# Gated cross-attention and FFN on one core: an own order of units for each engine, work moved off VectorE, and two batches' ctx turned in 32x32 blocks

## Chip, cores, metric

One core of one Trainium2 chip. The metric is device time in microseconds for one launch, the median of three runs. Engines: PE is TensorE (PEld its weight loads), DVE is VectorE, ACT ScalarE, POOL GpSimd, SP SyncE, which here only issues DMAs.

## What is computed

`x` has 4 batches of 256 tokens with 256 features, `ctx` 4 batches of 1601 rows of 256. Cut to what matters:

```python
h = layernorm(x)                                   # no scale or shift, eps 1e-5
scores = einsum('bsd,bmd->bsm', h, ctx) / sqrt(256)
scores = where(mask, scores, -1e30)
x = x + tanh(g_xattn) * (softmax(scores) @ ctx)    # zero where a batch has no valid row
a = e4m3(layernorm(x))
f = gelu(a @ e4m3(w_gating[0])) * (a @ e4m3(w_gating[1]))     # 256 -> 1024, bf16
x = x + tanh(g_ffn) * (e4m3(f) @ e4m3(w_linear))   # 1024 -> 256
```

## The kernel before

The 1024 tokens are 8 tiles j of 128, two per batch b. The ctx rows of a batch are 12 tiles of 128 and a tail of 65 rows; groups g = 0, 1, 2 hold four tiles each, g = 3 the tail. Both attention products are exact enough only if float32 values are split: `hi` is the value rounded to fp32r (a copy on ACT), `lo` the rest (value minus hi). Each product is then three: hi x hi, hi x lo, lo x hi.

All work is cut into units named by a letter and indices, in one written list (START, MIDDLE once per middle batch, END). Every engine walks this same list and does its own part of each unit, waiting on semaphores for the others:

- G, F, K: layernorm statistics of a batch (DVE), the power -0.5 (POOL, line 320), the normed `xn` (DVE, line 428, two per batch).
- R, Z: ctx group rounded by ACT (line 376, `chl` first half); its rest by POOL (line 334, second half, 1024 columns in one instruction).
- X, C, T: fills of a ring of three PSUM banks. PE transposes 128x128 pieces of `xn`, ctx or the probabilities through the identity (line 580); ACT evicts the bank rounded (line 369), DVE evicts the rest (line 436). C b:0 to b:5 are the six 512-column pieces of a batch (group times 2 + half of the features), C b:6 the tail.
- S j:c: score chunk c of tile j on PE (lines 595, 600, 601), six matmuls of 512 columns for c = 0, 1 and of 290 or 288 for c = 2, 3. M j:h: DVE adds the mask bias and takes the maximum of a half row (line 446, 1024 or 577 columns).
- E j:h: exponential on ACT (line 382). V j:g: probabilities times ctx on PE into bank `pv`: per ctx tile one matmul of 512 columns, hi against [hi | lo] (line 615), and one of 256, lo against hi (line 619).
- A: DVE adds the halves of the row sum (`rt`, line 463), inverts it, forms the factor `fo` (line 465) and adds both halves of `pv` to x (lines 467, 469).
- U, Q, L, N: second layernorm of a tile: statistics on DVE, power on POOL (line 326), the normed e4m3 values on DVE (line 479), N transposes (line 578) and DVE eviction (line 486).
- B: the mask turned to a bias on POOL (lines 311, 314), in an order that follows the ctx rows (row p x 12 + t sits on partition p of tile t).
- W, I: a 1024-column weight chunk rounded to the e4m3 grid: DVE makes the grid step (lines 496, 497), POOL adds and subtracts it (lines 342, 343). Six chunks: 0 to 3 gating, 4 and 5 linear.
- H 0 to 15: FFN hidden units (PE line 654, gelu on ACT line 394, product on DVE line 503); Y 0 to 7: projection (line 668) and final sum (DVE line 508).

`cn` (ctx as loaded) and `chl` exist twice, the turned ctx once. SP issues its DMAs in one fixed order; the loads of batch 2 wait for `c_lo` of batch 0.

Of the kernel before, what the change touches and what calls it, by code (L numbers as in the profile page):

```python
# [5 lines left out]
def gated_cross_attention_ffn(  # L6
# [55 lines left out]
    START = """
        G0 F0 B0 K0 R0:0 C0:0 C0:1 C0:2 X0 C0:3 C0:4 G1 S0:0 C0:5 C0:6 S0:1 F1 Z0:0 S0:2 S0:3 B1 M0:0 K1
        M0:1 G2 R0:1 Z0:1 E0:0 S1:0 G3 C1:0 S1:1 E0:1 T0:0 M1:0 S1:2 X1 R0:2 Z0:2 S1:3 T0:1 M1:1 T0:2
        V0:0 C1:1 R0:3 Z0:3 W0 E1:0 T0:3 V0:1 C1:2 C1:3 V0:2 R1:0 I0 Z1:0 F2 A0 C1:4 C1:5 R1:1 Z1:1 V0:3  # L80
        R1:2 Z1:2 C1:6 W1 E1:1 R1:3 Z1:3 I1 F3 B2 U0"""
# [9 lines left out]
    two_a_batch = "SMETVAUWI"

    def steps(text, batches=0):

        items = [(w[0], *(int(v) for v in w[1:].split(":"))) for w in text.split()]
        items = [(s[0], s[1] + batches * (QT if s[0] in two_a_batch else 1)) + s[2:] for s in items]
        return [s for s in items if s[0] != "B" or s[1] < B]
# [615 lines left out]
```

## Time and profile before

| | us |
|---|---|
| Median of three runs (lowest, highest) | 151.02 (150.79, 151.37) |
| Span of the profiled execution | 149.9 |
| PE busy | 130.0 |
| DVE busy | 126.9 |
| POOL busy | 74.8 |
| ACT busy | 71.2 |

The time beside the profiled execution's span is taken as the median, which lies 1.1 us above it. Busy time is the sum of an engine's instructions in the span; a DVE or POOL instruction that has started and then stands still counts as busy. In the rows, "x" is a count, the first pair after "|" is busy us in all and mean ns of one, then comes the idle time before the group and what ended it. Chain rows read: start, duration in us, what.

### The profile page before, as it was taken

The numbers are of one execution on the slowest core, as the hardware profiler recorded it, in microseconds if no ns is written. First come the engines' busy times: TensorE is split into PE (matmuls) and PEld (weight loads), VectorE is DVE, ScalarE is ACT, GpSimd is POOL, SyncE is SP. The second block draws the span as 40 slices with busy tenths as digits, with TensorE's granted clock in tenths as the row PEclk, the third lists the DMA queues.
The fourth block names the chain that finished last, engine by engine and source line by source line (L and its number), as shares of the span: only waits on it lengthen the run. The fifth ranks groups of instructions, "written<-read, shape, count | busy, mean of one in ns | idle before, by whom it ended". The sixth has DMA issues, their size and how long they took to land.

```text
span 149.9 us, 2277 instructions
## 1 busy us (share of the span) xinstructions
PE 130.0 (87%) x786; PEld 106.3 (71%) x786; DVE 126.9 (85%) x255; ACT 71.2 (47%) x131; POOL 74.8 (50%) x52
## 2 busy tenths in 40 slices
...
PEclk9978999999999999999699999995999999999999
...
GB/s 41 219 376 385 377 145 4 0 165 350 124 0 0 179 413 42 4 0 17 123 0 7 133 0 4 2 0 0 0 4 0 2 0 0 0 4 0 35 115 130
DMA packets 6754, 12.75 MB, mean 85 GB/s; under 512 B 852, under 2 KB 4696, under 8 KB 6744
## 3 DMA queue, kind: packets, MB, share of 16 engines
...
q10 hardware_dynamic: 288, 0.00, 0.1%
q14 instruction: 4, 0.03, 0.1%
...
## 4 chain that ended last, share of the span: by engine, by line
PE 50%; DVE 36%; DMA 5%; issue 4%; ACT 2%; SPq 1%; DVEq 0%
PE ring L580 12%; PE pv L615 11%; PE scores L654 7%; DVE act L428 6%; PE pv L619 6%; DVE wc L497 5%; DMA cn<-in_ctx_dram 5%; DVE wc L496 5%; DVE pT_lo L436 4%; PE ring L668 4%; DVE sp L446 3%; PE scores L600 3%; PE scores L601 3%; PE scores L595 3%; DVE cT_lo L436 2%
## 5 line engine op out<-in xcount | busy, mean ns | idle before, releaser
L334 POOL TENSOR_TENSOR chl<-cn,chl 128x1024 fp32r<-128x1024 f32 (+1 forms) x16 | 31.9, 2006 | 4.0 <-ACT chl L376 3.8
L369 ACT ACTIVATE pT_hi<-ring 128x512 fp32r<-128x512 f32 (+1 forms) x32 | 15.7, 514 | 36.3 <-PE ring L580 36.3
L615 PE MATMUL pv<-chl,pT_hi 128*128 128x512 f32 (+1 forms) x104 | 32.5, 427 | 0.0
L600 PE MATMUL scores<-cT_lo,xT_hi 128*128 128x512 f32 (+2 forms) x64 | 21.9, 350 | 6.6 <-DVE cT_lo L436 6.6
L601 PE MATMUL scores<-cT_hi,xT_lo 128*128 128x512 f32 (+2 forms) x64 | 21.7, 346 | 0.0
L436 DVE TENSOR_TENSOR pT_lo<-ring,pT_hi 128x512 fp32r<-128x512 f32 (+1 forms) x32 | 18.1, 582 | 3.7 <-ACT pT_hi L369 3.7
L619 PEld LDWEIGHTS pv<-chl,pT_lo 128*128 128x128 f32 (+1 forms) x104 | 16.9, 200 | 5.8 <-issue 1.9
L615 PEld LDWEIGHTS pv<-chl,pT_hi 128*128 128x128 f32 (+1 forms) x104 | 19.0, 199 | 2.7
L619 PE MATMUL pv<-chl,pT_lo 128*128 128x256 f32 (+1 forms) x104 | 18.3, 296 | 2.7 <-DVE pT_lo L436 2.7
L382 ACT ACTIVATE sp<-sp,nb 128x1024 f32<-128x1024 f32 (+1 forms) x16 | 15.4, 962 | 9.7 <-DVE nb L452 9.7
L580 PE MATMUL ring<-ident,sp 128*128 128x128 f32 (+1 forms) x104 | 16.5, 285 | 2.8 <-ACT sp L382 2.8
L595 PE MATMUL scores<-cT_hi,xT_hi 128*128 128x512 f32 (+2 forms) x64 | 18.7, 373 | 0.0
L342 POOL TENSOR_TENSOR ws<-ws,wc 128x1024 f32<-128x1024 f32 x6 | 13.0, 2160 | 11.4 <-DVE wc L497 11.4
L436 DVE TENSOR_TENSOR cT_lo<-ring,cT_hi 128x512 fp32r<-128x512 f32 (+1 forms) x28 | 16.7, 626 | 2.3 <-ACT cT_hi L369 2.0
L600 PEld LDWEIGHTS scores<-cT_lo,xT_hi 128*128 128x128 f32 x64 | 12.0, 188 | 8.6 <-DVE cT_lo L436 7.2
L580 PE MATMUL ring<-ident,cn 128*128 128x128 f32 (+1 forms) x104 | 15.4, 285 | 3.0 <-DMA cn<-in_ctx_dram 2.9
L369 ACT ACTIVATE cT_hi<-ring 128x512 fp32r<-128x512 f32 (+1 forms) x28 | 14.5, 550 | 6.4 <-PE ring L580 6.2
L580 PEld LDWEIGHTS ring<-ident,cn 128*128 128x128 f32 (+1 forms) x104 | 13.0, 151 | 4.2 <-issue 3.3
L580 PEld LDWEIGHTS ring<-ident,sp 128*128 128x128 f32 (+1 forms) x104 | 13.1, 147 | 4.0 <-issue 3.3
L326 POOL TENSOR_TENSOR rstd<-ve,half_pow 128x2 f32<-128x2 f32 x4 | 2.8, 698 | 26.1 <-DVE ve L425 26.1
L446 DVE CUSTOM_DVE_ANT_0 sp<-scores,bias 128x1024 f32<-128x1024 f32 (+1 forms) x16 | 15.7, 981 | 0.1
L376 ACT ACTIVATE chl<-cn 128x1024 fp32r<-128x1024 f32 (+1 forms) x16 | 14.3, 899 | 1.2 <-DMA cn<-in_ctx_dram 1.2
...
## 6 DMA issues: line engine op xcount, KB each, us to landing
...
```

Source lines behind the costliest of these rows:

```text
L334: nc.gpsimd.tensor_tensor(chl[b % 2][0:parts, t0:t1, D:2 * D], cn[b % 2][0:parts, t0:t1, :], chl[b % 2][0:parts, t0:t1, 0:D].bitcast(f32), ...
L369: nc.scalar.activation(dst, bank_view(f, size), ACT.Copy).then_inc(hi_ready, 1)
L376: nc.scalar.activation(chl[b % 2][0:parts, t0:t1, 0:D], cn[b % 2][0:parts, t0:t1, :], ACT.Copy).then_inc(c_hi, 1)
L382: nc.scalar.activation(sp[:, j % 2, cols], sp[:, j % 2, cols], ACT.Exp, bias=nb[:, j:j + 1], scale=SCALE, accum_out=rs[:, j, h:h + 1]).the ...
L436: nc.vector.tensor_tensor(dst, bank_view(f, size), hi.bitcast(f32), ALU.subtract).then_inc(freed, 1)
L446: nc.vector.tensor_tensor_reduce(out=sp[:, j % 2, cols], in0=banks[:, at_col:at_col + cols.stop - cols.start], in1=bias[:, b % 2, cols], s ...
L580: last = nc.tensor.transpose(dst, src, ident[0:parts, 0:parts])
L595: nc.tensor.matmul(dst, xT_hi[:, j, k, :], cT_hi[:, k, cols], start=(k == 0), stop=False)
L600: nc.tensor.matmul(dst, xT_hi[:, j, k, :], cT_lo[:, k, cols], start=False, stop=False)
L601: last = nc.tensor.matmul(dst, xT_lo[:, j, k, :], cT_hi[:, k, cols], start=False, stop=(k == KD - 1))
L615: return nc.tensor.matmul(pv[:, :], pT_hi[0:parts, t, :], chl[b % 2][0:parts, t, :], start=(t == 0), stop=(t == NT - 1))
L619: nc.tensor.matmul(pv[:, 0:D], pT_lo[0:parts, t, :], chl[b % 2][0:parts, t, 0:D], start=False, stop=False)
```

## The change

- Each engine gets its own written order of units. SP's order interleaves the loads by ctx group (lower-case letters: x, c, m, w loads, b blocks, o stores).
- DVE to ACT: the first layernorm is now `x` centred only (mean minus x, on ACT), and the factor is applied as scale of the exponential; the second layernorm's values, the N eviction, and the absolute value of a weight chunk times 2^20 (`w_abs`, 1024 columns) go to ACT. The two exponentials of a tile become one of 1601 columns, so `rt` goes.
- DVE to POOL: F is now four small operations, Q three per tile instead of one per batch, and v, the validity factor, one per tile.
- POOL's `chl` rest and weight rounding are issued in 256-column pieces: 4 for a group, 8 for a weight chunk.
- The grid step on DVE is one maximum over 1024 float32 columns instead of two passes over bf16.
- `pv` sums everything in 256 columns: hi x hi and hi x lo are two matmuls of 256 columns; DVE adds `pv` once.
- Batches 2 and 3, groups 0 to 2: instead of six C fills (24 transposes) a second load of ctx, `load_blocks`, puts 32x32 blocks so that one DVE transpose of 32x32 blocks per group (D, 1024 columns) gives the turned ctx; ACT rounds it (1024 columns), POOL forms the rest in four pieces. Their row order changes too, so the bias of these batches is one plain instruction.
- `cn` exists once; group 2 and the tail of `chl` and of the turned ctx exist once, groups 0 and 1 twice. 22 warm-up matmuls instead of 18.

```diff
+    BLOCKED = (2, 3)
...
+    SP_ORDER = steps("""
+        x0 c0:1 c0:0 m0 c0:2 c0:3 x1 c1:1 w0 m1 m2 w1 c1:3 x2 c1:0 c1:2 b2 c2:1 c2:0 w2 m3 w3 b3 c2:3 w4 c2:2
+        c3:0 c3:3 c3:1 w5 c3:2 o3 o0 o1 o2 o4 o5 o6 o7""")
+    ACT_ORDER = steps("""
+        R0:1 C0:3 K0 C0:2 X0 C0:0 C0:1 R0:0 R0:3 C0:5 C0:6 C0:4 J R0:2 K1 W0 C1:2 X1 E0 C1:3 T0:0 T0:1 R1:1 T0:2
+        R1:0 K2 C1:6 T0:3 C1:0 C1:1 W1 C1:5 C1:4 E1 T1:0 T1:2 T1:1 D2:0 X2 E2 W2 D2:1 T1:3 L0 R2:1 T2:1 R1:2
+        T2:0 R1:3 D2:2 T2:3 T2:2 E3 T3:0 R2:0 T3:1 T3:2 K3 C2:6 W3 X3 T3:3 D3:0 E4 D3:1 R2:2 T4:0 R2:3 D3:2 T4:1
+        T4:3 T4:2 L1 R3:0 E5 C3:6 T5:2 T5:1 R3:1 T5:0 T5:3 L2 N0 E6 W4 L3 R3:3 T6:2 T6:0 R3:2 T6:1 E7 T6:3 L4 N1
+        T7:0 H0 T7:1 L5 T7:3 H1 T7:2 W5 L6 H2 N2 H3 L7 H4 H5 N3 H6 H7 H8 H9 H10 H11 H12 H13 H14 H15""")
+    DVE_ORDER = steps("""
+        G0 C0:3 C0:2 X0 C0:0 C0:1 G1 C0:5 C0:4 C0:6 M0:0 M0:1 C1:2 W0 X1 C1:3 G2 T0:0 T0:1 M1:0 T0:2 O0 C1:6
+        M1:1 T0:3 C1:0 C1:1 C1:5 C1:4 A0 W1 M2:0 T1:0 D2:0 D2:1 M2:1 T1:2 U0 T1:1 D2:2 M3:0 O2 X2 T1:3 W2 O1 A1
+        T2:1 T2:0 M3:1 M4:0 T2:3 U1 T2:2 G3 T3:0 A2 D3:0 T3:1 O3 C2:6 T3:2 M4:1 X3 D3:1 M5:0 W3 T3:3 D3:2 T4:0
+        U2 A3 M5:1 T4:3 T4:1 T4:2 M6:0 T5:2 C3:6 T5:1 U3 T5:3 O4 A4 O5 T5:0 M6:1 U4 M7:0 A5 U5 T6:0 M7:1 T6:1
+        T6:2 O6 W4 T6:3 T7:0 A6 H0 O7 T7:1 U6 T7:2 H1 W5 T7:3 A7 U7 H2 H3 H4 H5 H6 H7 H8 H9 H10 H11 H12 Y0 H13
+        H14 Y1 H15 Y2 Y3 Y4 Y5 Y6 Y7""")
+    POOL_ORDER = steps("""
+        Z0:1 B0 F0 Z0:3 Z0:0 Z0:2 B1 F1 F2 v0 I0 Z1:1 Z1:0 v1 I1 D2:0 v2 Q0 B2 D2:1 Z1:2 Z1:3 v3 D2:2 I2 Z2:1
+        Z2:0 Q1 F3 D3:0 D3:1 v4 B3 Z2:3 Z2:2 Q2 v5 D3:2 I3 Q3 Z3:1 Z3:0 Q4 Q5 v6 Z3:2 v7 Z3:3 I4 Q6 Q7 I5""")
+    PE_ORDER = steps("""
+        C0:3 C0:2 X0 C0:0 C0:1 S0:1 C0:5 C0:6 C0:4 S0:0 C1:2 S0:2 S0:3 X1 S1:0 C1:3 S1:1 T0:0 T0:1 S1:3 S1:2
+        T0:2 C1:6 V0:0 V0:1 T0:3 C1:0 C1:1 S2:1 C1:5 C1:4 V0:2 V0:3 S2:0 T1:0 T1:2 T1:1 S2:3 S3:1 S2:2 X2 S3:0
+        V1:0 S3:2 T1:3 T2:1 V1:1 V1:2 V1:3 S3:3 T2:0 S4:1 T2:3 T2:2 S4:0 V2:0 V2:1 V2:2 T3:0 V2:3 T3:1 T3:2 S5:0
+        C2:6 S4:2 V3:0 X3 S4:3 T3:3 V3:1 S5:1 V3:2 S5:3 T4:0 V3:3 T4:1 S5:2 S6:0 T4:2 T4:3 S6:1 V4:0 V4:1 V4:2
+        C3:6 T5:2 T5:1 V4:3 S7:0 T5:0 S6:2 T5:3 S6:3 S7:1 N0 V5:0 V5:1 V5:2 T6:0 V5:3 T6:2 S7:2 S7:3 T6:1 V6:0
+        N1 V6:1 T6:3 V6:2 T7:0 T7:1 H0 V6:3 H1 T7:3 T7:2 V7:0 V7:1 V7:2 V7:3 N2 H2 H3 H4 H5 N3 H6 H7 H8 H9 H10
+        Y0 H11 H12 H13 H14 H15 Y1 Y2 Y3 Y4 Y5 Y6 Y7""")
...
+            def load_ctx(b, g):
+                if b >= 1:
+                    sp_eng.wait_ge(c_lo, pool_z[("Z", b - 1, g)])
+                    if g == NG - 1:
+                        sp_eng.wait_ge(filled, pe_fill[("C", b - 1, KD * g)])
...
+                t0, t1, _ = group(g)
+                rows = ctx_2048[b, 0:NF * P, :].rearrange("(t p) d -> p t d" if b in BLOCKED else "(p t) d -> p t d", t=NF)
+                sp_eng.dma_start(cn[:, t0:t1, :], rows[:, t0:t1, :]).then_inc(c_in[g], 16)
+
+            def load_blocks(b):
+                earlier = [dve_d[s] for s in turns if s[1] < b]
+                if earlier:
+                    sp_eng.wait_ge(turned, max(earlier))
+                src = ctx_2048[b, 0:NF * P, :].rearrange("(m q) (k i d) -> k i q m d", q=Q, k=KD, d=Q)
+                for k in range(KD):
+                    for i in range(P // Q):
+                        sp_eng.dma_start(cb[Q * i:Q * (i + 1), k, :, :], src[k, i]).then_inc(b_in, 16)
...
+                for t in range(t1 - t0):
+                    ins = nc.gpsimd.tensor_tensor(chl(b, g)[0:parts, t, D:2 * D], cn[0:parts, t0 + t, :],
+                                                  chl(b, g)[0:parts, t, 0:D].bitcast(f32), ALU.subtract)
+                ins.then_inc(c_lo, 1)
...
+            def turned_rest(b, g):
+                pool.wait_ge(d_hi, act_d[("D", b, g)])
+                slot = turns.index(("D", b, g)) % 2
+                for k in range(KD):
+                    for a in range(0, BANK, D):
+                        ins = nc.gpsimd.tensor_tensor(cT(b, g, False)[:, k, a:a + D], cr[:, slot, k, a:a + D],
+                                                      cT(b, g, True)[:, k, a:a + D].bitcast(f32), ALU.subtract)
+                ins.then_inc(d_lo, 1)
...
+                pool.wait_ge(wg_ready, dve_w[("W", i)])
+                for a in range(0, HID, D):
+                    ins = nc.gpsimd.tensor_tensor(ws[:, i % 2, a:a + D], ws[:, i % 2, a:a + D], wg[:, a:a + D], ALU.add)
+                link(ins)
+                for a in range(0, HID, D):
+                    ins = nc.gpsimd.tensor_tensor(wq[:, i, a:a + D], ws[:, i % 2, a:a + D], wg[:, a:a + D], ALU.subtract)
+                ins.then_inc(w_ready, 1)
...
+                    ins = nc.scalar.activation(xc[:, j, :], xs[:, j, :], ACT.Identity, bias=mv[:, j, 0:1], scale=-1.0)
...
+            def turned_hi(b, g):
+                wait_ctx_read(actor, b, g)
+                actor.wait_ge(turned, dve_d[("D", b, g)])
+                nc.scalar.activation(cT(b, g, True), cr[:, turns.index(("D", b, g)) % 2, :, :], ACT.Copy).then_inc(d_hi, 1)
...
+            def turn(b, g):
+                n = turns.index(("D", b, g))
+                if g == 0 or turns[n - 1][1] != b:
+                    dve.wait_ge(b_in, 16 * KD * (P // Q) * (sorted(BLOCKED).index(b) + 1))
+                if n >= 2:
+                    dve.wait_ge(d_lo, pool_d[turns[n - 2]])
+                nc.vector.transpose(cr[:, n % 2, :, :],
+                                    cb[:, :, GT * GT * g:GT * GT * (g + 1), :].rearrange("p k m d -> p k (m d)")).then_inc(turned, 1)
...
+            def factor(j):
+                dve.wait_ge(exp_ready, act_e[("E", j)])
+                link(nc.vector.reciprocal(ri[:, j:j + 1], rs[:, j:j + 1]))
+                dve.wait_ge(vt_ready, pool_v[("v", j)])
+                nc.vector.tensor_scalar(fo[:, j:j + 1], ri[:, j:j + 1], vt[:, j:j + 1], None, ALU.mult).then_inc(fo_ready, 1)
+
             def add_attention(j):
-                if j == 0:
-                    dve.wait_ge(tg_ready, 1)
-
-                dve.wait_ge(nb_ready, j + 1)
-                nc.vector.tensor_scalar(vt[:, j:j + 1], nb[:, j:j + 1], 0.5 * NEG * SCALE, tg[:, 0:1],
-                                        ALU.is_lt, ALU.mult)
-                dve.wait_ge(exp_ready, 2 * (j + 1))
-                link(nc.vector.tensor_tensor(rt[:, j:j + 1], rs[:, j, 0:1], rs[:, j, 1:2], ALU.add))
-                link(nc.vector.reciprocal(ri[:, j:j + 1], rt[:, j:j + 1]))
-                link(nc.vector.tensor_tensor(fo[:, j:j + 1], ri[:, j:j + 1], vt[:, j:j + 1], ALU.mult))
-                dve.wait_ge(pv_done, j + 1)
-                link(nc.vector.scalar_tensor_tensor(out=xs[:, j, :], in0=pv[:, D:2 * D], scalar=fo[:, j:j + 1],
-                                                    in1=xs[:, j, :], op0=ALU.mult, op1=ALU.add))
+                dve.wait_ge(fo_ready, dve_o[("O", j)])
+                dve.wait_ge(weighed, pe_weigh[("V", j, NG - 1)])
...
+                nc.vector.tensor_scalar(wg[:, :], wg[:, :], GRID_MIN * 2.0 ** 20, None, ALU.max).then_inc(wg_ready, 1)
...
+                for t in range(t0, t1):
+                    for part in range(2):
+                        nc.tensor.matmul(pv[:, 0:D], pT_hi[0:parts, t, :], ctx[0:parts, t - t0, D * part:D * (part + 1)],
+                                         start=(t == 0 and part == 0), stop=False)
+                pe.wait_ge(freed, dve_lo[("T", j, g)])
+                for t in range(t0, t1):
+                    last = nc.tensor.matmul(pv[:, 0:D], pT_lo[0:parts, t, :], ctx[0:parts, t - t0, 0:D],
+                                            start=False, stop=(t == NT - 1))
+                last.then_inc(weighed, 1)
```

## Rows read from the trace of the kernel before

**Rows 1.** The page: busy us (share of the span); PE's clock in 40 slices.

```profile
PE 130.0 (87%) x786; PEld 106.3 (71%) x786; DVE 126.9 (85%) x255; ACT 71.2 (47%) x131; POOL 74.8 (50%) x52
...
PEclk9978999999999999999699999995999999999999
```

**Rows 2.** The page: chain that ended last, by engine.

```profile
PE 50%; DVE 36%; DMA 5%; issue 4%; ACT 2%; SPq 1%; DVEq 0%
```

**Rows 3.** Groups by line and form, DVE.

```profile
L436 DVE TENSOR_TENSOR cT_lo<-ring,cT_hi 128x512 fp32r<-128x512 f32 x24 | 15.7, 684 | 2.3 <-ACT cT_hi L369 2.0
...
L428 DVE TENSOR_SCALAR act<-xs,mv,rstd 128x256 f32<-128x256 f32 x8 | 10.5, 1353 | 0.8 <-POOL rstd L320 0.8
...
L446 DVE CUSTOM_DVE_ANT_0 sp<-scores,bias 128x1024 f32<-128x1024 f32 x8 | 9.7, 1215 | 0.1
...
L497 DVE TENSOR_SCALAR wc<-wc 128x1024 bf16<-128x1024 bf16 x6 | 8.3, 1379 | 0.2
...
L496 DVE TENSOR_SCALAR wc<-ws 128x1024 uint16<-128x1024 uint16 x6 | 7.3, 1216 | 0.0
...
L463 DVE TENSOR_TENSOR rt<-rs 128x1 f32<-128x1 f32 x8 | 5.6, 698 | 0.0
```

**Rows 4.** Timeline of DVE, 30 to 75 us: start us, us, what.

```profile
34.01 2.00 DVE L465 TENSOR_TENSOR fo<-ri,vt 128x1 f32<-128x1 f32 x1
...
46.13 3.20 DVE L428 TENSOR_SCALAR act<-xs,mv,rstd 128x256 f32<-128x256 f32 x2
```

**Rows 5.** Timeline of POOL, same columns.

```profile
33.84 2.15 POOL L343 TENSOR_TENSOR wq<-ws,wc 128x1024 bf16<-128x1024 f32 x1
...
47.03 2.15 POOL L343 TENSOR_TENSOR wq<-ws,wc 128x1024 bf16<-128x1024 f32 x1
```

**Rows 6.** Chain that ended last, in order of time: start us, us, what.

```profile
51.57 0.47 PE scores L595 x2
...
53.85 0.27 PE scores L595 x2
...
57.85 1.31 PE ring L580 x12
...
59.16 0.93 PE pv L615 x4
...
60.09 0.48 PE pv L619 x4
...
120.04 0.22 PE ring L578 x4
...
127.12 1.74 PE scores L654 x8
```

**Rows 7.** ACT: its timeline to 45 us; then a group by form.

```profile
7.81 1.06 ACT L376 ACTIVATE chl<-cn 128x1024 fp32r<-128x1024 f32 x1 [1.21 <-DMA cn<-in_ctx_dram]
...
L376 ACT ACTIVATE chl<-cn 65x256 fp32r<-65x256 f32 x4 | 1.6, 410 | 0.0
```

**Rows 8.** Groups by line and form, POOL.

```profile
L334 POOL TENSOR_TENSOR chl<-cn,chl 128x1024 fp32r<-128x1024 f32 x12 | 28.9, 2428 | 3.3 <-ACT chl L376 3.3
...
L343 POOL TENSOR_TENSOR wq<-ws,wc 128x1024 bf16<-128x1024 f32 x6 | 13.5, 2249 | 0.5
...
L311 POOL TENSOR_SCALAR bias<-mrow 128x1536 bf16<-128x1536 uint8 x4 | 9.2, 2299 | 6.3 <-DMA mrow<-in_mask_BxS_bk_dram 4.5 <-DVE mx L446 1.6
...
L334 POOL TENSOR_TENSOR chl<-cn,chl 65x256 fp32r<-65x256 f32 x4 | 3.0, 739 | 0.6 <-ACT chl L376 0.5
...
L326 POOL TENSOR_TENSOR rstd<-ve,half_pow 128x2 f32<-128x2 f32 x4 | 2.8, 698 | 26.1 <-DVE ve L425 26.1
```

**Rows 9.** Timeline of SP's queue.

```profile
49.64 1.33 SPq L254 DMA_DIRECT2D cn<-in_ctx_dram  x3
```

**Rows 10.** DMA queues, 0 to 20 us, then 68 to 84 us: packets, MB, share of 16 engines.

```profile
q10 hardware_dynamic: 288, 0.00, 0.7%
...
q1 hardware_dynamic: 1000, 1.01, 22.8%
```

More of the change, by code:

```diff
@@ L91, in gated_cross_attention_ffn @@
[L91 to L97, printed above, removed]
-    order = steps(START) + [s for b in range(B - 2) for s in steps(MIDDLE, b)] + steps(END)
-    fills = [s for s in order if s[0] in "XCTN"]
-    at = {f: i for i, f in enumerate(fills)}
```

569 lines of the change are left out of this document (315 added, 254 removed).

## The prediction

> **What bounds the kernel now.** I read the page first: PE is busy for 130.0 us of the span and DVE for 126.9, so two engines are near full, while ACT (71.2) and POOL (74.8) have room [rows 1]. The chain that ended last agrees: PE half, DVE 36% [rows 2]. A busy DVE is not a working DVE here, though. The `xn` operation of line 428 takes 1353 ns on average for 256 columns, and line 463, one element per partition, 698 ns [rows 3]. The two timelines side by side say why. The one-element `fo` starts at 34.01 and lasts 2.00 us [rows 4]; POOL's 1024-column operation starts at 33.84 and lasts 2.15, so both end at 36.0 [rows 5]. The `xn` pair at 46.13 ends at 49.3, with POOL's operation of 47.03 [rows 4, 5]. DVE stands still until POOL has finished, up to a whole 2.2 us operation.
>
> The Trainium skill ("SBUF — State Buffer", SBUF: two separate sides) calls this an exclusive lock on a port pair, held for a whole instruction and taken by GpSimd and by DVE operations with two SBUF inputs or in a two-port mode. The two pairs of ends agree with it.
>
> PE's own work, at the pace it has when nothing holds it: a transpose 0.109 us (1.31/12), a 512-column score matmul 0.235, a 289-column one 0.135 (0.27/2), a 512-column `pv` matmul 0.233 (0.93/4), a 256-column one 0.12 (0.48/4), an FFN unit 0.87 (1.74/2) [rows 6]. Up to the end of the last attention tile (127.1, where the FFN runs on alone [rows 6]) that is 224 transposes (4 x 26 of ctx, 8 x 13 of probabilities, 16 of `xn`) 24.4, scores 8 x (12 x 0.235 + 12 x 0.135) = 35.3, `pv` 8 x 13 x 0.353 = 36.7, and 2.4 for H0, H1 and three N fills (0.22 each [rows 6]): 98.8 us. The first ctx group is there at 7.8 [rows 7], so in 119.3 us PE lacked 20.5. From 127.1 to the end are 22.8 us, which PE's own 14 FFN units and 64 projection matmuls fill.
>
> **The change part by part.** The sum is against the profiled execution's span of 149.9; the median of the runs, 151.02, is 1.1 above it, and I add that 1.1.
>
> *PE.* 48 transposes (24 each in batches 2 and 3) go: -5.2, leaving 93.6. Splitting the 512-column `pv` matmul into two of 256 costs 2 x 0.12 against 0.233: nothing. Its extra weight loads I cost at nothing too, since the `pT_lo` matmuls load weights before each 256 columns and still run at 0.12 [rows 6]; were it not so, 104 loads would each show. Four more warm-up matmuls lie before the first data.
>
> *DVE.* Gone: 8 `xn` (10.5), 6 mask operations of line 496 (7.3), 8 `rt` (5.6), 12 `cT_lo` evictions (12 x 0.684 = 8.2) [rows 3]; 31.6 in all, and some 36 short ones besides. Added: 6 turns of 1024 columns. No row has a 32x32 turn. Bounds: 0.68, what an eviction of half the columns takes, and 2.4, twice the 1.215 of the 1024-column mask pass; I take 1.2, the same columns [rows 3]: +7.2. The grid operation stays one pass of 1024 (1.38 today [rows 3]), now waiting for at most a 256-column piece. DVE falls to about 100 or less: no longer a bound.
>
> *ACT.* It takes on 16 passes of 256 columns (0.41), 4 of 512 and 6 of 1024 (1.06 each at most) [rows 7]: +6.6 +4.2 +6.4; the 6 turned evictions of 1024 replace 12 of 512. About 88 of 140 us: cover enough.
>
> *POOL.* Here the price is paid. A 1024-column subtraction takes 2.43 us; a 256-column one (on 65 partitions) 0.74 [rows 8]. Four pieces cost between 2.43, if their start-up hides in one another, and 2.96; I take 2.7. Likewise a weight chunk (two passes of 2.2 [rows 8]): 4.3 to 5.4, I take 4.9. Line 320's successor has four small operations, line 326's three per tile; the power takes 0.70 [rows 8] and I give the sets 1.35 and 1.2. In POOL's order, up to the unit Z3:2 that V6:2 waits for: 12 Z x 2.7 = 32.4; three tails 2.2; 6 D x 2.7 = 16.2; 4 masks x 2.5 (2.30 and its tail [rows 8]) = 10.0; 4 F 5.4; four weight chunks 19.6; 6 Q 7.2; 7 v 1.4. Sum 94.4, within about 108 in all against 74.8 now. POOL can start when ScalarE has rounded the first group: 7.8 + 1.06 = 8.9 [rows 7]. I allow 3 us of waiting early (mask, first maxima), so Z3:2 is done at 106.3.
>
> *The sum.* PE has 84.1 us of work ahead of V6:2 by the same prices, so it can be there by 7.8 + 84.1 + 14 of idling, just about in time. From V6:2 it has 9.5 left (V6:2 1.4, T7 1.4, H0 and H1 1.7, the rest of V 5.0), then the 22.8 of the end, which the change leaves as it is: 106.3 + 9.5 + 22.8 = 138.6, and with 1.1 **139.7 us**.
>
> *DMA of the blocks.* Each batch's 1536 rows come again in 128-byte runs, 12288 of them, through 8 DMAs that SP issues at 0.44 each (1.33/3 [rows 9]). Price of a run: a packet of 4 bytes shows as 0.7% of 16 engines in 20 us over 288, 7.8 ns; one of 1010 bytes as 22.8% in 16 us over 1000, 58 ns [rows 10]. Bounds 6.0 us (7.8) and 44.6 us (58) per batch; on the line between, 128 bytes is 14 ns, 10.8 us, which I take, as 128 lies near the small end. Block load 2 is queued behind c1:2, which waits for Z0:2: POOL's sum there gives 21.6. With 3 us of ctx ahead of it and 2 us to land it is there by 37. POOL reaches D2:0 at 42.4 plus 2 of waiting; with turn and eviction ahead, the blocks are wanted at 42. Slack 5 us, or a price of 20.6 ns. Block load 3 waits for D2:2 (about 48, past w3, which waits for I1) and is wanted at 71: slack 10, or 27 ns. At my price both hide. If not, DVE stands at D2:0 with T1:1, U0, M3:0 and all behind it, and ACT and POOL stand behind the same unit.
>
> **The rivals.**
> *A, the pieces are cheap* (2.43 per four, 4.3 per chunk, small operations overlapping): POOL's sum is 9 us less and PE with some 10 us of idling, half of today's, sets the end: 7.8 + 93.6 + 10 + 22.8 + 1.1 = 135. For it: nothing excludes that the start of one piece hides in the piece before; against it: the 65-partition row, far above a quarter of 2.43.
> *B, the waits between engines stay.* PE idles its 20.5 for other reasons than DVE's load (a unit goes PE, ACT, DVE, PE): 7.8 + 93.6 + 20.5 + 22.8 + 1.1 = 145.8. Pieces at 2.96 and 5.4 give nearly the same, 146.4. For it: many hand-offs remain, and in three stretches PE's granted clock falls below its 2.4 GHz (slices at 7, 6 and 5 tenths [rows 1]); against it: DVE had no slack at all to hide a hand-off.
> *C, slower: the blocks come late.* The price of a 128-byte run decides. Total delay is (0.768 p - 15.8) + (0.768 p - 20.8) us, each not below zero, p in ns. It eats the gain of 11.3 at p = 31. At the upper bound, 58 ns, the kernel takes 192. At 33 ns, a run priced as one four times as long on the same line, it takes 139.7 + 9.5 + 4.5 = 154. For it: no row shows a short run from HBM; the 4-byte packets repeat one address. Against it: the price must be more than twice the one read off the line.
> The Trainium skill ("DMA: Bandwidth & Descriptors", Specifications) puts 512 bytes as the least transfer at full rate, since below it the engine reads, modifies and writes. By that rule a 128-byte run costs like a 512-byte one, which is this rival; the trace has no such run to show it.
>
> The skill ("GPSIMD Engine Reference", Engine selection) also advises against two-input elementwise work on GpSimd, as about twice as slow as DVE. The rows bear it out (2428 ns for 1024 columns against 684 for 512 [rows 3, 8], 1.8 times). The change adds 6 units of it, which is why I let POOL set the sum.
>
> **How the numbers follow.** A run-to-run difference below about 0.5% can't be told from none. Chances: the forecast (136 to 143) 0.42; A (131 to 136) 0.18; below 131 0.03; B (143 to 150.2) 0.20; no difference 0.03; C 0.14. Faster 0.83, same 0.03, slower 0.14. The range 131 to 150 leaves out C, no difference and the tail below: 0.20.
>
> **What would show it.** Right: POOL busy over 100 us with hardly a gap between 20 and 105; DVE near 85 to 100 us, no one-element operation above 0.7 us; PE about 5 us less dense work, and waiting for POOL's `chl` or `cT_lo` late in attention; block loads landing within 15 us of issue and DVE's turns near 1.2 us. Wrong: DVE idle ahead of the first turn for a DMA (C); POOL with gaps while PE waits on ACT or DVE (B); a 256-column piece near 0.6 us start to start and PE hardly waiting (A).

## The result, and the profile after

| | time, us (lowest to highest) | ratio to before |
|---|---|---|
| before | 151.19 (150.79 to 152.72) | |
| changed | 146.37 (144.94 to 147.56) | 0.971 [0.964, 0.978] |
| forecast | 139.7 (131 to 150) | |

Faster, as forecast, but by 4.8 us where 11.3 had been forecast. A second measurement gave 147.04 us. The profiled execution is the slowest of its four, 147.56 us with a span of 145.7, and so is that of the second measurement (147.73, span 145.9), both at a mean granted clock of 0.94 where the other six had 0.95 to 0.99 and spans of 143.1 to 145.2, so what is read from these two traces stands for them alone. The time lies 1.8 to 1.9 us above the span in every run here, not 1.1.

The page of the changed kernel: busy time by engine, PE's clock, and the chain that ended last by engine and by line.

```profile
PE 126.3 (87%) x846; PEld 108.0 (74%) x846; DVE 85.0 (58%) x186; ACT 84.6 (58%) x135; POOL 114.4 (79%) x186
...
PEclk9955999999758999999999999999999599999999
...
POOL 67%; PE 21%; DMA 4%; issue 3%; ACT 1%; DVE 0%; SPq 0%; POOLq 0%
POOL chl_a L433 16%; POOL chl_b L433 10%; POOL wq L455 8%; POOL ws L452 8%; POOL cTl_a L444 8%; PE scores L777 7%; PE ring L793 5%; DMA cn<-in_ctx_dram 4%; POOL cTl_b L444 4%; POOL bias L406 3%; PE pv L753 3%; POOL rstd L422 3%; POOL bias L403 2%; POOL sc L394 2%; POOL vt L416 2%
```

DVE went from 126.9 to 85.0 us and left the chain, where it had 36% [rows 1, 2]; POOL went from 74.8 to 114.4 and holds 67% of it (54% in the second profile, with 3% for DVE). PE's busy time fell by 3.7 only, and it idles about as much as before (19.4 us of the span). The bound moved from DVE to POOL.

POOL's groups by line and form, changed kernel (columns as in [rows 8]):

```profile
L433 POOL TENSOR_TENSOR chl_a<-cn,chl_a 128x256 fp32r<-128x256 f32 x32 | 22.8, 748 | 7.1 <-ACT chl_a L517 7.0
L455 POOL TENSOR_TENSOR wq<-ws,wg 128x256 bf16<-128x256 f32 x24 | 16.9, 733 | 0.5
L452 POOL TENSOR_TENSOR ws<-ws,wg 128x256 f32<-128x256 f32 x24 | 16.8, 729 | 0.1
L433 POOL TENSOR_TENSOR chl_b<-cn,chl_b 128x256 fp32r<-128x256 f32 x16 | 12.2, 795 | 0.1
L444 POOL TENSOR_TENSOR cTl_a<-cr,cTh_a 128x256 fp32r<-128x256 f32 x16 | 11.8, 774 | 0.1
L444 POOL TENSOR_TENSOR cTl_b<-cr,cTh_b 128x256 fp32r<-128x256 f32 x8 | 5.2, 686 | 0.0
...
L406 POOL TENSOR_SCALAR bias<-mrow 128x1536 bf16<-128x1536 uint8 x2 | 4.7, 2338 | 0.2
L403 POOL TENSOR_SCALAR bias<-mrow 128x1601 bf16<-128x1601 uint8 x2 | 3.1, 1536 | 0.2
L416 POOL TENSOR_SCALAR vt<-nb,lim,tg 128x1 f32<-128x1 f32 x8 | 3.0, 379 | 0.1
```

After its first 7 us of waiting nothing holds POOL up before 118 us, where the last ctx rest is long done: the idle column is near zero. The 12 ctx groups cost 22.8 + 12.2 = 35.0 us against 28.9 before [rows 8].

PE's timeline around the unit V6:2, changed kernel: start us, us, what, then the idle time before it.

```profile
111.97 1.28 PE L753 MATMUL pv<-chl_b,pT_hi 128*128 128x256 f32 x8 [2.58 <-POOL chl_b L433]
113.04 1.05 PE L757 MATMUL pv<-chl_b,pT_lo 128*128 128x256 f32 x4
...
121.46 1.10 PE L753 MATMUL pv<-chl_b,pT_hi 128*128 128x256 f32 x8
```

Stretches of the changed kernel: busy time (count) of PE, PEld, DVE, ACT, POOL, then PE's granted clock, DMA share and GB/s.

```profile
112.00:114.00 2.00, 2.00 (x13) 2.00 (x14) 0.00 (x0) 0.00 (x0) 1.92 (x4) 0.75 0.01 4
114.00:116.00 2.00, 2.00 (x10) 1.69 (x9) 0.32 (x1) 0.93 (x2) 1.92 (x4) 0.50 0.03 8
116.00:118.00 2.00, 2.00 (x11) 1.18 (x10) 0.51 (x2) 1.89 (x3) 2.00 (x4) 0.90 0.00 0
```

PE waits 2.58 us for POOL's rest of ctx group 3:2, which is the wait the forecast was built on. Behind it the clock is granted at half (0.50, that is 1.2 GHz) for some 3 us: four 256-column matmuls take 1.05 us where the same four take 0.63 elsewhere.

POOL and DVE in the changed kernel around one of DVE's grid steps (`wg`):

```profile
21.17 1.10 DVE L645 TENSOR_SCALAR wg<-wg 128x1024 f32<-128x1024 f32 x1
...
21.67 1.21 POOL L433 TENSOR_TENSOR chl_b<-cn,chl_b 128x256 fp32r<-128x256 f32 x1
```

This one piece of 256 columns takes 1.21 us where its neighbours take some 0.73. Each of the six grid steps has such a drawn-out POOL instruction beside it, and up to Z3:2 no other is drawn out: pieces of 1.21, 1.19, 1.36 and 1.17 us, and a power of 1.08 instead of 0.56 us.

The DMA queue of the changed kernel from 51 to 62 us, while the second block load runs (columns as in [rows 10]), and the page's issues (count, KB each, us to landing):

```profile
q1 hardware_dynamic: 12490, 1.64, 93.0%
```

```profile
cb<-in_ctx_dram SPq DMA_DIRECT2D x16, 192.0 KB, 3.7
```

A 128-byte run takes 0.93 x 16 x 11 us / 12490 = 13.1 ns. DVE's groups in the changed kernel:

```profile
L611 DVE STREAM_TRANSPOSE cr<-cb 128x1024 f32<-128x1024 f32 x6 | 7.3, 1232 | 5.7 <-POOL cTl_a L444 5.7
...
L645 DVE TENSOR_SCALAR wg<-wg 128x1024 f32<-128x1024 f32 x6 | 4.9, 818 | 0.0
...
L635 DVE TENSOR_SCALAR fo<-ri,vt 128x1 f32<-128x1 f32 x8 | 1.7, 214 | 3.2 <-POOL vt L416 3.0
```

The turn takes 1.23 us and waits for POOL, never for a DMA. The one-element `fo`, 2.00 us long at its worst before [rows 4], takes 0.21.

### The profile page after: what moved, and what is told of

The parts are those of the page before. It is cut to its first block, busy times and chain, and to the rows that moved or that the text cites. A ratio compares the mean times of both kernels' runs of the same rounds, so it can differ in the third digit from the quotient of the medians.

```text
span 145.7 us, 2596 instructions
## 1 busy us (share of the span) xinstructions
PE 126.3 (87%) x846; PEld 108.0 (74%) x846; DVE 85.0 (58%) x186; ACT 84.6 (58%) x135; POOL 114.4 (79%) x186
## 3 DMA queue, kind: packets, MB, share of 16 engines
HBM read 14.72 MB, written 1.05 MB: 108 GB/s over the span
## 4 chain that ended last, share of the span: by engine, by line
POOL 67%; PE 21%; DMA 4%; issue 3%; ACT 1%; DVE 0%; SPq 0%; POOLq 0%
POOL chl_a L433 16%; POOL chl_b L433 10%; POOL wq L455 8%; POOL ws L452 8%; POOL cTl_a L444 8%; PE scores L777 7%; PE ring L793 5%; DMA cn<-in_ctx_dram 4%; POOL cTl_b L444 4%; POOL bias L406 3%; PE pv L753 3%; POOL rstd L422 3%; POOL bias L403 2%; POOL sc L394 2%; POOL vt L416 2%
## 5 line engine op out<-in xcount | busy, mean ns | idle before, releaser
L433 POOL TENSOR_TENSOR chl_a<-cn,chl_a 128x256 fp32r<-128x256 f32 x32 | 22.8, 748 | 7.1 <-ACT chl_a L517 7.0
L502 ACT ACTIVATE pT_hi<-ring 128x512 fp32r<-128x512 f32 (+1 forms) x32 | 15.8, 512 | 16.7 <-PE ring L722 16.6
L753 PE MATMUL pv<-chl_a,pT_hi 128*128 128x256 f32 x128 | 18.3, 285 | 1.0 <-issue 1.0
L753 PEld LDWEIGHTS pv<-chl_a,pT_hi 128*128 128x128 f32 x128 | 16.4, 189 | 1.5 <-issue 1.2
L455 POOL TENSOR_TENSOR wq<-ws,wg 128x256 bf16<-128x256 f32 x24 | 16.9, 733 | 0.5
L452 POOL TENSOR_TENSOR ws<-ws,wg 128x256 f32<-128x256 f32 x24 | 16.8, 729 | 0.1
L753 PE MATMUL pv<-chl_b,pT_hi 128*128 128x256 f32 (+1 forms) x80 | 12.9, 292 | 4.2 <-POOL chl_b L433 4.2
L739 PE MATMUL scores<-cTl_a,xT_hi 128*128 128x512 f32 x32 | 13.2, 413 | 3.7 <-POOL cTl_a L444 2.6
L433 POOL TENSOR_TENSOR chl_b<-cn,chl_b 128x256 fp32r<-128x256 f32 (+1 forms) x20 | 15.1, 782 | 0.3
L522 ACT ACTIVATE sp<-sp,nb,sc 128x1601 f32<-128x1601 f32 x8 | 13.8, 1724 | 0.4 <-DVE nb L628 0.2
L740 PE MATMUL scores<-cTh_a,xT_lo 128*128 128x512 f32 x32 | 12.9, 402 | 0.0
```

What stands on the lines that cost most here:

```text
L433: ins = nc.gpsimd.tensor_tensor(chl(b, g)[0:parts, t, D:2 * D], cn[0:parts, t0 + t, :], chl(b, g)[0:parts, t, 0:D].bitcast(f32), ALU.subtract)
L452: ins = nc.gpsimd.tensor_tensor(ws[:, i % 2, a:a + D], ws[:, i % 2, a:a + D], wg[:, a:a + D], ALU.add)
L455: ins = nc.gpsimd.tensor_tensor(wq[:, i, a:a + D], ws[:, i % 2, a:a + D], wg[:, a:a + D], ALU.subtract)
L502: nc.scalar.activation(dst, bank_view(f, size), ACT.Copy, scale=-1.0 if f[0] == "X" else 1.0).then_inc(hi_ready, 1)
L522: nc.scalar.activation(sp[:, j % 2, 0:K], sp[:, j % 2, 0:K], ACT.Exp, bias=nb[:, j:j + 1], scale=sc[:, j:j + 1], accum_out=rs[:, j:j + 1]) ...
L739: nc.tensor.matmul(dst, xT_hi[:, b % 2, q, k, :], lo[:, k, :], start=False, stop=False)
```

## The experiments

Every kernel computes the whole output unless said otherwise. "Place" is the start of V6:2 on PE, the first matmul that reads the rest of ctx group 3:2; "tail" is the span less the place.

| kernel | time, us | ratio to before | POOL busy | place | tail |
|---|---|---|---|---|---|
| changed | 146.37 | 0.971 [0.964, 0.978] | 114.4 | 111.97 | 33.7 |
| e10 changed, once more | 147.04 | 0.971 [0.962, 0.980] | 114.7 | 112.19 | 33.7 |
| e1 all of POOL's work whole | 133.76 | 0.888 [0.882, 0.894] | 101.2 | 100.31 | 32.0 |
| e9 only ctx rests whole | 139.14 | 0.923 [0.919, 0.927] | 108.7 | 105.21 | 32.1 |
| e5 ctx rests in 128-column pieces | 152.27 | 1.007 [1.003, 1.012] | 121.3 | 118.42 | 32.1 |
| e2 turned rests on DVE | 135.47 | 0.899 [0.892, 0.906] | 102.3 | 101.65 | 32.0 |
| e4 e2, and the rest whole | 130.78 | 0.869 [0.863, 0.874] | 90.7 | 97.01 | 32.0 |
| e11 ctx rest 3:2 ahead of Q5, v6 | 145.08 | 0.957 [0.952, 0.963] | 114.2 | 109.99 | 33.7 |
| e3 before, POOL in pieces | 141.05 | 0.936 [0.929, 0.944] | 85.8 | | |
| e6 changed, without blocks | 155.98 (152.94 to 156.00) | unclear | 99.2 | | |
| e7 e6, POOL's work whole | 152.41 | 1.005 [1.000, 1.010] | 88.6 | | |
| e8 e7, fills spread out | 160.04 | 1.058 [1.048, 1.067] | 88.9 | | |

**e1: the changed kernel with 1024-column instructions on POOL.** Its three loops become one instruction each:

```diff
-                for t in range(t1 - t0):
-                    ins = nc.gpsimd.tensor_tensor(chl(b, g)[0:parts, t, D:2 * D], cn[0:parts, t0 + t, :],
-                                                  chl(b, g)[0:parts, t, 0:D].bitcast(f32), ALU.subtract)
+                ins = nc.gpsimd.tensor_tensor(chl(b, g)[0:parts, :, D:2 * D], cn[0:parts, t0:t1, :],
+                                              chl(b, g)[0:parts, :, 0:D].bitcast(f32), ALU.subtract)
```

> The changed kernel with GpSimd's work in 1024-column instructions again (ctx rest, turned rest, both passes of a weight chunk); all orders as changed. Theory 'GpSimd paces': its work ahead of Z3:2 shrinks by 12 x 0.39 + 6 x 0.39 + 4 x 1.3 = 12 us, so that VectorE's longest wait for it grows from one piece to one instruction, but VectorE is 58% busy and only its six grid passes take part: 137 to 142 us, GpSimd busy about 100. Rival 'locks': the six grid passes and what is queued behind them wait up to 2.4 us each, and the pieces were what made the schedule work: 146 or more. Rival 'hand-offs': the waits between engines set the time whatever GpSimd's load is: within 1 us of 146.

Measured: 133.76 us, 12.6 less than the changed kernel and beyond what was expected. The page (busy, then chain) and POOL's groups of e1:

```profile
PE 121.7 (92%) x846; PEld 104.7 (79%) x846; DVE 88.9 (67%) x186; ACT 84.4 (64%) x135; POOL 101.2 (77%) x96
...
PE 55%; POOL 28%; DVE 6%; DMA 4%; issue 2%; ACT 1%; SPq 0%; POOLq 0%; DVEq 0%; ACTq 0%
```

```profile
L432 POOL TENSOR_TENSOR chl_a<-cn,chl_a 128x1024 fp32r<-128x1024 f32 x8 | 19.0, 2393 | 6.5 <-ACT chl_a L510 6.4
L449 POOL TENSOR_TENSOR wq<-ws,wg 128x1024 bf16<-128x1024 f32 x6 | 14.3, 2390 | 0.5
L448 POOL TENSOR_TENSOR ws<-ws,wg 128x1024 f32<-128x1024 f32 x6 | 14.3, 2380 | 0.1
```

Up to the place POOL saves 6.4 us on the 12 ctx groups (35.0 to 19.0 + 9.6), 1.9 on the turned rests and 3.4 on four weight chunks: 11.7, and the place moves by 11.7; the tail is 1.7 shorter besides. DVE pays for it with `wg` at 1479 instead of 818 ns, +4.0 us in all, which it can afford.

**e9: only the ctx rests whole** (the edit shown above, alone).

> The changed kernel with only the ctx rest in 1024-column instructions (turned rest and weight passes stay in pieces). With the 128-column run this is one dose in both directions. 'GpSimd paces': Z3:2 ends 12 x 0.42 = 5 us earlier, 106.9, and the time is 140 to 142. 'Locks': 146 or more.

Measured: 139.14 us, a little below the range. The place moves by 6.8 us; the groups give 35.0 - 28.5 = 6.5.

**e5: the ctx rests in 128-column pieces.**

```diff
-                    ins = nc.gpsimd.tensor_tensor(chl(b, g)[0:parts, t, D:2 * D], cn[0:parts, t0 + t, :],
-                                                  chl(b, g)[0:parts, t, 0:D].bitcast(f32), ALU.subtract)
+                    for a in range(0, D, P):
+                        ins = nc.gpsimd.tensor_tensor(chl(b, g)[0:parts, t, D + a:D + a + P], cn[0:parts, t0 + t, a:a + P],
+                                                      chl(b, g)[0:parts, t, a:a + P].bitcast(f32), ALU.subtract)
```

> The changed kernel with the ctx rest in 128-column pieces (8 a group, 2 for the tail) in place of 256; nothing else. The other direction of the same dose: a piece of 128 columns should take about 0.45 us, a group 3.6 in place of 2.8, so 12 x 0.8 + 3 x 0.2 = 10 us more GpSimd work ahead of Z3:2. 'GpSimd paces': 154 to 158 us. If something else set the time as well: less than 150.

POOL's groups of e5:

```profile
L434 POOL TENSOR_TENSOR chl_a<-cn,chl_a 128x128 fp32r<-128x128 f32 x64 | 26.9, 466 | 6.4 <-ACT chl_a L518 6.3
...
L434 POOL TENSOR_TENSOR chl_b<-cn,chl_b 128x128 fp32r<-128x128 f32 x32 | 14.4, 493 | 0.1
```

Measured: 152.27 us, 5.9 more than the changed kernel where some 10 had been expected: the pieces cost 26.9 + 14.4 - 35.0 = 6.3, and the place moves by 6.45. The added size was overestimated, the slope of one between POOL's work and the time holds. A group of 1024 columns takes 2.39 us as one instruction, 2.78 as four (from 16.79 to 19.57 in the changed kernel's timeline of POOL, where nothing disturbs it) and 26.9 / 8 = 3.36 as eight: each further instruction adds 0.13 to 0.14 us.

**e2: the turned rests on DVE.** POOL's 24 pieces go; DVE gets one instruction per group, in its order behind the turn.

```diff
+            def turned_rest(b, g):
+                dve.wait_ge(d_hi, act_d[("D", b, g)])
+                slot = turns.index(("D", b, g)) % 2
+                nc.vector.tensor_tensor(cT(b, g, False), cr[:, slot, :, :],
+                                        cT(b, g, True).bitcast(f32), ALU.subtract).then_inc(d_lo, 1)
```

> The changed kernel with the rest of the six turned groups formed by VectorE in one 1024-column instruction each, not by GpSimd in four pieces. GpSimd loses 16.9 us of work ahead of Z3:2, VectorE gains about 7.5. 'GpSimd paces': 137 to 141 us, then PE with 5 to 10 us less idle time. 'Hand-offs': within 1 us of 146, since each turned group still goes VectorE, ScalarE and back. 'Locks': VectorE's new two-input passes stand behind pieces, up to 0.7 us each, which is little.

Measured: 135.47 us, below the range of 'GpSimd paces'. Taking 17.0 us of work from POOL moved the place by 10.3 only. Two POOL groups of e2 show the larger part of the rest, and its timeline of DVE and POOL where it comes from:

```profile
L434 POOL TENSOR_TENSOR chl_b<-cn,chl_b 128x256 fp32r<-128x256 f32 x16 | 12.7, 822 | 1.6 <-ACT chl_b L507 1.5
L417 POOL TENSOR_SCALAR vt<-nb,lim,tg 128x1 f32<-128x1 f32 x8 | 6.0, 754 | 0.1
```

```profile
46.15 1.82 DVE L607 TENSOR_TENSOR cTl_a<-cr,cTh_a 128x1024 fp32r<-128x1024 f32 x1
...
46.86 1.35 POOL L417 TENSOR_SCALAR vt<-nb,lim,tg 128x1 f32<-128x1 f32 x1
```

The one-element `vt` takes 754 instead of 379 ns in the mean. Three of the eight take 1.24 to 1.55 us, and each of these ends 0.24 to 0.26 us after one of DVE's new two-input instructions (here 48.21 after 47.97): POOL stands still until DVE has finished, as DVE did behind POOL before. `vt` costs 3.0 us more in all, other instructions beside DVE's new ones about 2, and one wait for ACT 1.5.

**e4: e2 with the ctx rests and weight passes whole.**

> Both of the above edits of the changed kernel: the turned rest on VectorE, ctx rest and weight passes in 1024-column instructions. GpSimd has about 27 us less to do and is no bound. 'GpSimd paces': PE sets the time, 134 to 138 us. 'Locks': VectorE's twelve locked 1024-column passes wait up to 2.4 us each, so it is no better than the better of the two alone. 'Hand-offs': within 1 us of 146.

The page of e4, and V6:2 in its timeline of PE:

```profile
PE 119.0 (92%) x846; PEld 102.2 (79%) x846; DVE 93.8 (73%) x192; ACT 84.2 (65%) x135; POOL 90.7 (70%) x90
...
PE 53%; POOL 17%; DVE 17%; issue 4%; DMA 4%; ACT 1%; SPq 0%; DVEq 0%; ACTq 0%; POOLq 0%
```

```profile
97.01 1.19 PE L746 MATMUL pv<-chl_b,pT_hi 128*128 128x256 f32 x8
```

Measured: 130.78 us, better than expected and the fastest version of the study. V6:2 has no wait behind POOL any more, and no engine but PE holds over a fifth of the chain.

**e3: the kernel before, with nothing but the 256-column pieces** (ctx rests and weight passes).

> The kernel before with one part of the change: GpSimd's ctx rest and weight passes in 256-column pieces. If VectorE's standing behind 1024-column instructions was what cost (some 25 us of its busy time), its busy time falls by 10 to 18 us, GpSimd's rises by about 12, and the time falls to 143 to 147. Rival: that standing was hidden behind PE anyway, or pieces lock VectorE out as often as whole ones: 150 to 152.

DVE's groups of e3, and its chain:

```profile
L505 DVE TENSOR_SCALAR wc<-wc 128x1024 bf16<-128x1024 bf16 x6 | 5.3, 878 | 0.2
L504 DVE TENSOR_SCALAR wc<-ws 128x1024 uint16<-128x1024 uint16 x6 | 5.1, 845 | 0.0
L436 DVE TENSOR_SCALAR act<-xs,mv,rstd 128x256 f32<-128x256 f32 x8 | 4.8, 637 | 0.8 <-POOL rstd L320 0.8
...
L471 DVE TENSOR_TENSOR rt<-rs 128x1 f32<-128x1 f32 x8 | 2.0, 248 | 0.0
```

```profile
PE 67%; POOL 16%; DMA 9%; issue 2%; ACT 1%; SPq 1%; DVE 1%; POOLq 0%
```

Measured: 141.05 us, faster than the whole change and than expected: below the range of 143 to 147. Against [rows 3], `xn` falls from 1353 to 637 ns, `rt` from 698 to 248, the grid passes from 1379 and 1216 to 878 and 845; DVE's busy time falls by 16.9 us, and DVE leaves the chain. POOL pays 11.0 us more and has room for it. PE's idle time falls from 19.9 to 11.0 us and its busy time by 2.8: the clock, which fell in three stretches before [rows 1], stays up in e3's profile. How much of the 10 us is the clock is not split. Pieces of the same size thus do opposite things:

| | POOL whole | POOL in 256-column pieces |
|---|---|---|
| kernel before | 151.19 | 141.05 (-10.1) |
| changed kernel | 133.76 | 146.37 (+12.6) |

**e6, e7, e8: without the blocks.** In e6 batches 2 and 3 get their 12 C fills back at places in PE's, ACT's and DVE's orders near those of the removed D units; e7 is e6 with POOL's work whole; e8 is e7 with the fills spread earlier and batch 3's group 1 loaded ahead of its tail.

```diff
-    BLOCKED = (2, 3)
+    BLOCKED = ()
...
-        V1:0 S3:2 T1:3 T2:1 V1:1 V1:2 V1:3 S3:3 T2:0 S4:1 T2:3 T2:2 S4:0 V2:0 V2:1 V2:2 T3:0 V2:3 T3:1 T3:2 S5:0
+        V1:0 S3:2 T1:3 T2:1 V1:1 V1:2 V1:3 S3:3 T2:0 C2:2 C2:3 S4:1 T2:3 T2:2 C2:0 C2:1 S4:0 V2:0 V2:1 V2:2 T3:0 V2:3 T3:1 T3:2 S5:0
```

> The changed kernel without the block loads and turns: batches 2 and 3 get their six 512-column C fills back (PE transposes, ScalarE and VectorE evict), placed where the turned groups were used; pieces and all other orders as changed. GpSimd loses 16.9 us ahead of Z3:2, PE gains 5.2, VectorE about nil. 'GpSimd paces': 136 to 142 us, so the blocks cost more than they bring in this schedule. Rival 'PE is the scarce one': 148 or more.

> The same without blocks, and GpSimd's work in 1024-column instructions. GpSimd has some 90 us in all and no longer paces; PE has 5.2 us more to do than with blocks. If PE sets the time once GpSimd has room, 134 to 138 us, above the 130.8 of the kernel with blocks whose rest VectorE forms. If blocks bring nothing at all: 131 or less.

> Again no blocks and 1024-column GpSimd instructions, with the C fills of batches 2 and 3 spread one or two at a time between other units and placed earlier, and the load c3:1 ahead of c3:3. If the 152 us of the first order was only its placement (each score chunk right behind its own fills, PE waiting for ScalarE and VectorE to evict them), this comes to 134 to 140, PE's 5.2 us above the versions with blocks. If the fills cannot come earlier, because the single ctx buffer lets their loads in only after GpSimd's rest of the batch before: 145 or more, and then blocks are worth more than the 5.2 us of PE.

Measured: 155.98, 152.41 and 160.04 us, each far above the range of the theory it was to test. e6 and e8 fall where their rivals had put them (148 or more, 145 or more); for e7 nothing above 138 had been foreseen. The chains of e6 and of e7, and one wait of e8 (us in total, times, longest):

```profile
PE 58%; POOL 15%; DVE 11%; ACT 5%; issue 4%; DMA 4%; SPq 0%; ACTq 0%; DVEq 0%; POOLq 0%
```

```profile
PE 57%; POOL 15%; DVE 11%; issue 6%; ACT 5%; DMA 4%; SPq 0%; ACTq 0%; DVEq 0%; POOLq 0%
```

```profile
PE ring L699 <- DMA cn<-in_ctx_dram: 13.0, 3, 6.9
```

POOL is off the bound and PE still slower. Against the changed kernel, e6's PE is 5.7 us longer busy and 2.8 longer idle. Against e1, which has blocks and whole instructions too, e7's is 11.9 us longer busy and 8.2 longer idle; its chain goes partly through DVE (11%) and ACT (5%), whose evictions the fills wait for. Moving the fills forward (e8) made it worse and had PE wait 13.0 us for ctx, since `cn` exists once and can't be loaded before its last reader is done, which is e8's second theory. Blocks have a buffer of their own, `cb`, and escape this. So in these three orders the kernel without blocks is some 19 us slower than e1 at best (152.41 to 133.76), far more than the 5.2 us of transposes. What the blocks themselves are worth is not shown: the fills' places were mine and perhaps poor, and a double `cn` was not tried.

**e10: the changed kernel once more.**

> The changed kernel once more, unaltered, for a second profile and the time beside the same runs of the kernel before. In the first profile V6:2 started at 111.97 and the span ended 33.7 us later, where the variants with less GpSimd work took 32.0 from that unit on. If the 1.7 us are PE's clock falling after its wait for GpSimd, they come with a granted clock below 1 in 110 to 118 us; if they are chance of one execution, the rest is 32.0 to 32.3 here. Time 145 to 147.

Measured: 147.04 us, place 112.19 with the same wait of 2.58 us, tail 33.7. Its stretch from 114 to 116 us:

```profile
114.00:116.00 2.00, 2.00 (x11) 1.97 (x11) 0.00 (x0) 0.52 (x1) 2.00 (x4) 0.50 0.00 0
```

The half clock comes again at the same place, so it is not the chance of one execution. That every execution has it is not shown: the other six are 0.7 to 2.6 us shorter and have no trace. In e5's trace half clock follows a wait of 2.14 us too, a little earlier in PE's order (V6:0):

```profile
111.77 1.20 PE L754 MATMUL pv<-chl_a,pT_hi 128*128 128x256 f32 x8 [2.14 <-issue]
```

```profile
114.00:116.00 2.00, 2.00 (x10) 2.00 (x10) 0.86 (x2) 0.00 (x0) 2.00 (x5) 0.50 0.00 0
```

**e11: POOL forms the rest 3:2 earlier.**

```diff
-        ... Z3:1 Z3:0 Q4 Q5 v6 Z3:2 v7 Z3:3 I4 Q6 Q7 I5""")
+        ... Z3:1 Z3:0 Q4 Z3:2 v6 Q5 v7 Z3:3 I4 Q6 Q7 I5""")
```

> The changed kernel, whose GpSimd now forms the rest of ctx group 3:2 before the second layernorm's small operations of tile 5 and the validity factor of tile 6. That unit is then ready 1.2 + 0.4 = 1.6 us earlier (110.3 instead of 111.9 us) and TensorE waits for it about 1.0 instead of 2.6 us. Theory 1 (GpSimd's sum sets the time, and TensorE's half clock behind that place comes from its long wait): the clock stays at 1.00 there, 32.0 to 32.2 us follow instead of 33.7, span 142.3 to 142.8, time 143.7 to 144.6. Theory 2 (the half clock has another cause and stays): only the 1.6 us, span 144.1 to 144.5, time 145.5 to 146.3. Rival (tiles 5 and 6 were just in time, and their delayed factors stop ScalarE or VectorE): no gain, 146.5 to 148.

PE's timeline and one stretch of e11:

```profile
109.99 1.21 PE L753 MATMUL pv<-chl_b,pT_hi 128*128 128x256 f32 x8 [0.51 <-POOL chl_b L433]
111.04 0.63 PE L757 MATMUL pv<-chl_b,pT_lo 128*128 128x256 f32 x4
...
117.84 1.10 PE L753 MATMUL pv<-chl_b,pT_hi 128*128 128x256 f32 x8
...
120.99 0.38 PE L757 MATMUL pv<-chl_b,pT_lo 65*128 65x256 f32 x1 [1.34 <-DVE pT_lo L603]
```

```profile
110.00:112.00 2.00, 2.00 (x17) 2.00 (x18) 1.01 (x3) 0.82 (x2) 1.73 (x5) 1.00 0.04 8
```

Measured: 145.08 us (144.40 to 145.54), beside 147.04 (145.34 to 147.73) for the changed kernel on the same chip: 2.0 us less, with ranges that touch. With a wait of 0.51 instead of 2.58 us the clock stays at 1.00 and the four `pT_lo` matmuls are back at 0.63; V7:2 comes 117.84 - 109.99 = 7.85 us after V6:2, in the changed kernel 121.46 - 111.97 = 9.49. So theory 1 is right about the clock at this place, and the half clock cost 1.6 us in the changed kernel's trace. The time lies between the ranges of theory 1 (to 144.6) and theory 2 (from 145.5) all the same: V7:2 starts 3.6 us earlier, but the span is only 2.0 shorter. A new wait stands at 120.99, for DVE's last `pT_lo`. DVE's order has the grid step of weight chunk 5 ahead of it, and the chain back from there is ScalarE's absolute value, then POOL's chunk 4:

```profile
ACT wg L544 <- POOL wq L455: 2.1, 1, 2.1
DVE wg L645 <- ACT wg L544: 1.9, 1, 1.9
...
PE pv L757 <- DVE pT_lo L603: 1.3, 1, 1.3
```

(Waits of e11 from 117 us on.) Chunk 4 can't be done sooner, because POOL's sum up to there is the same. POOL bounds at two places one behind the other.

## Why the prediction was right and wrong

**Right: what sets the end.** "POOL sets the sum", with PE waiting for group 3:2 at V6:2, and POOL without gaps. In e1, e9, e5, e2 and e4 the tail behind the place is 32.0 to 32.1 us, and the forecast had 9.5 + 22.8 = 32.3. Where the place moved, the time moved with it, from 130.8 to 152.3 us.

**Right: the side prices.** The turn, 1.2 forecast, 1.23 measured; the 128-byte run, 14 against 13.1 ns; DVE 85.0 in "85 to 100"; ACT 84.6 against 88. The split `pv` matmuls cost next to nothing: eight of 256 columns in 111.04 - 109.99 = 1.05 us (e11), 0.13 each where 0.12 was taken. (One slip in the working changes nothing: the scores come to 35.5 us by the prices given, not 35.3.)

**Wrong: "Four pieces cost between 2.43 and 2.96; I take 2.7", and "4.3 to 5.4, I take 4.9".** Here the forecast's size failed. The term's place was right, its size was not:

| POOL from its start at 8.90 us to the end of Z3:2, us | forecast | measured |
|---|---|---|
| 12 ctx groups | 32.4 | 35.6 |
| 6 turned rests | 16.2 | 16.9 |
| 4 weight chunks | 19.6 | 22.8 |
| 4 masks | 10.0 | 8.7 |
| 4 F, 6 Q, 7 v | 14.0 | 16.6 |
| tails | 2.2 | 2.4 |
| waiting | 3.0 | 0 |
| sum | 97.4 | 103.0 |

(Measured from each unit's start to the next unit's start, so with the short gaps between them.) The mean of a group, 35.6 / 12 = 2.97, stands at the upper bound, but only part of that is start-up. Undisturbed, the group of four takes 2.78, near the 2.7 taken. Of the other 0.19 (2.2 us in twelve groups), 1.4 is a term that the forecast didn't have: in three of the groups one piece runs beside DVE's grid step and takes some 0.45 us longer. With one turned rest and one power that meet the same, it is 2.5 us of POOL's 103.0. The forecast had read that DVE stands behind POOL, and put nothing down for POOL behind DVE. The weight chunk lies above its bound, at 5.70. Its price came from passes with a bf16 second input (2.25 us, [rows 8]); the change makes that input float32, and the same pass whole then takes 2.38 to 2.39 (e1), where 2.2 had been taken. Reading only the column count of the row, and not its types, hid 0.3 to 0.4 us per chunk; the rest is six further instructions at 0.13. The small operations are dearer too: v costs 0.38 us, not 0.2, F 1.5 instead of 1.35 and Q 1.3 instead of 1.2. Some of this cancelled: the masks were 1.3 us cheaper, and the 3.0 us of waiting didn't come.

**Wrong: the stretch from V6:2 to V7, 11.4 us instead of 9.5.** The forecast gave PE its best pace there. After a wait of 2.58 us it got the half clock in both profiles: 1.6 us, shown by e11 and by the tails of the other kernels (waits of 0, 0.7, 0.9, 1.6 and 1.7 us there, and tails of 32.0 to 32.1). The other 0.3 is price: e1 takes 9.8 us there at the full clock.

Together: POOL 103.0 - 97.4 = +5.6, the stretch +1.9, the end 22.3 for 22.8, -0.5: +7.0, which leads from the forecast's span of 138.6 to the profile's 145.7 within 0.1. The time beside the span is 0.7 us more than the forecast's 1.1, and the median, 146.37, lies 1.2 below the profiled execution; so the forecast of 139.7 was 6.7 short.

**Rival B** stood at 145.8 and so had the number, but its reason, that hand-offs between engines stay, is not what happened: POOL holds 67% of the chain (54% in the second profile), and e1 removes 12.6 us without touching an order. Its second sentence, pieces at 2.96 and 5.4 giving 146.4, was close to the true case (2.97 and 5.70), though that it meets the median is partly luck: the half clock, the small operations, the masks and the waiting are not in it. It should have been a rival of its own with a high chance, since the 65-partition row (0.74) spoke for it. **Rival A** is refuted by the same rows (0.70 us from piece to piece, not 0.6).

**Rival C** is refuted: 13.1 ns a run against the 31 it needed. The Trainium skill ("DMA: Bandwidth & Descriptors", Specifications) puts 512 bytes as the least transfer at full rate, and by the reading I gave it a 128-byte run would cost like one of 512 bytes. The trace disagrees with that reading: 512 bytes in 13.1 ns would be 625 GB/s over 16 engines, while the highest slice of this kernel's own profile moves 372. That short runs move less per second is borne out: 150 GB/s in that window.

**What the forecast did not ask:** which of the change's parts pay. It counted the pieces almost as a price alone, after it had itself read that DVE stood behind POOL for whole instructions. e3 gives the answer it could have looked for: in the old kernel shortening that standing was worth 10 us, more than the whole change. And as the change takes DVE off the bound, the pieces lose their use and keep their price. What the separate order of each engine and the work moved from DVE to ACT are worth by themselves was not tried.
